# Local attention's first three slots between the MLP's last steps, and TensorE multiplying an identity in the opening

## The reference, cut to what matters

```python
def _reference_tuple_inner(inputs, ...):                 # the first layer
    x = _layernorm(inputs, ln1_g, ln1_b)
    attn_out, extra_loss = _lha_attention(x, Wq, Wk, Wv, Whq, Whk, Wo)   # 16 heads of 8
    x = attn_out + inputs
    y = _layernorm(x, ln2_g, ln2_b)
    y = jax.nn.relu(jnp.einsum('bsd,dm->bsm', y, W1) + b1)              # 128 -> 512
    y = jnp.einsum('bsm,md->bsd', y, W2) + b2
    return (x + y, extra_loss)
...
def _layer(x, wqkv, qs, ksc, wo, lg, lb, w1, b1, w2, b2):   # twice, the local layers
    h = shift_token(x)                       # half of the features from the token before
    q, k, v = jnp.split(h @ wqkv, 3, axis=-1)                            # 8 heads of 64
    q = l2norm(q) * qs
    k = l2norm(k) * ksc
    q, k = rotary_xpos(q, k)
    o = local_attention(q, k, v)             # windows of 64, each sees itself and the one before
    x = x + o @ wo
    ...                                      # shift, layer norm, gated MLP
```

## Time and profile before

| | |
|---|---|
| median of 3 runs | 1442.46 us (1438.47 to 1443.82) |
| the profiled execution | 1443.05 us, span 1441.3 us |
| mean granted TensorE clock | 0.964 of full |
| PE busy | 1268.8 us (88%) |
| DVE busy | 1084.5 us (75%) |
| ACT busy | 1007.7 us (70%) |
| POOL busy | 824.9 us (57%) |

### The profile page before, as it was taken

One profiled execution on the slowest core, in us unless ns is written; L12 is line 12 of the kernel. 1 busy time (PEld: TensorE's weight loads), 2 busy tenths in 40 slices (PEclk: granted clock), 3 DMA queues, 4 the chain that ended last, 5 costly groups with the idle time before them and its releaser, 6 DMA issues.

```text
span 1441.3 us, 27920 instructions
## 1 busy us (share of the span) xinstructions
PE 1268.8 (88%) x9636; PEld 643.8 (45%) x9636; DVE 1084.5 (75%) x1927; ACT 1007.7 (70%) x2327; POOL 824.9 (57%) x1020
## 2 busy tenths in 40 slices
PE   4489989899899977896799999988987999999898
PEld 1122222222222212365366666665434666666554
DVE  6678888888888865334499999994448999999644
ACT  4656767666676656774489999984348999999632
POOL 3466667676667631133778888860048787887100
PEclk9579999999999999998799999999999999999999
DMA  6533333333333320001111111120001111111001
GB/s 165 97 60 66 59 72 69 60 66 60 68 73 60 66 53 1 1 1 33 26 27 32 30 27 28 28 60 8 0 22 42 28 27 27 29 30 28 2 22 37
DMA packets 161119, 60.87 MB, mean 42 GB/s; under 512 B 139690, under 2 KB 152788, under 8 KB 160980
## 3 DMA queue, kind: packets, MB, share of 16 engines
q1 hardware_dynamic: 160980, 59.09, 19.3%
HBM read 8.60 MB, written 2.10 MB: 7 GB/s over the span
## 4 chain that ended last, share of the span: by engine, by line
PE 29%; ACT 11%; DVE 8%; issue 4%; POOL 2%; ACTq 0%; DVEq 0%; POOLq 0%
ACT la_s L1859 8%; PE la_ring L1480 6%; PE la_ring L1492 3%; PE la_s L1515 3%; PE la_pT L1589 3%; DVE la_prob L1748 2%; PE la_pT L1528 2%; PE la_m L1663 2%; PE la_ring L1577 2%; PE la_s L1579 1%; PE la_pT L1579 1%; PE la_s L1577 1%; ACT la_v_own L1901 1%; PE la_s L1507 1%; PE la_o L1544 1%
## 5 line engine op out<-in xcount | busy, mean ns | idle before, releaser
L785 DVE TENSOR_REDUCE row_max<-max_ps 128x2 f32<-128x1024 f32 x256 | 312.8, 1222 | 77.3 <-PE max_ps L481 75.8
L890 ACT ACTIVATE prob<-scores_ps 128x1024 f32<-128x1024 f32 x256 | 261.8, 1023 | 145.3 <-PE scores_ps L459 141.8
L1859 ACT ACTIVATE la_s<-la_s,la_bias,la_inv 128x128 f32<-128x128 f32 x512 | 223.2, 443 | 7.0 <-DVE la_bias L1736 7.0
L2010 POOL TENSOR_TENSOR la_turned<-la_raw,lw_rot 128x1024 f32<-128x1024 f32 x64 | 150.8, 2356 | 117.1 <-PE la_ring L1492 72.1
L1480 PE MATMUL la_ring<-lw_wqkv,la_hT 128*128 128x512 f32 x384 | 202.6, 638 | 15.5 <-DVE la_swapped L1711 6.8
L459 PE MATMUL scores_ps<-stack 128*128 128x512 f16 x512 | 155.7, 386 | 36.6 <-ACT prob L890 36.2
L2016 POOL TENSOR_TENSOR la_turned<-la_turned,la_swapped 128x1024 f32<-128x1024 f32 x64 | 150.6, 2354 | 5.0
L495 PE MATMUL heads_ps<-prob,XT 128*32 128x512 f32 x1024 | 137.9, 611 | 0.0
L481 PE MATMUL max_ps<-stack 24*128 24x512 f16 x512 | 102.7, 398 | 31.1 <-DVE row_max L785 19.1
L459 PEld LDWEIGHTS scores_ps<-stack 128*128 128x128 f16 x512 | 34.5, 97 | 203.8 <-ACT prob L890 148.9
L1067 POOL TENSOR_TENSOR cl<-cl,cl_inv 128x512 f32<-128x512 f32 x60 | 62.8, 1047 | 103.3 <-DVE cl_inv L691 103.3
(11 more groups left out here) (186 smaller groups left out, 2748.7 us busy)
## 6 DMA issues: line engine op xcount, KB each, us to landing
la_v_back<-la_v_own SPq DMA_DIRECT2D x112, 128.0 KB, 2.3
X<-in_x SPq DMA_DIRECT2D x8, 256.0 KB, 5.0
stack<-stack_tok SPq DMA_TRANSPOSE x128, 3.2
out<-X SPq DMA_DIRECT2D x8, 256.0 KB, 2.3
lw_wqkv<-in_wqkv SPq DMA_DIRECT2D x2, 768.0 KB, 4.3
lw_rot<-in_rot SPq DMA_DIRECT2D x2, 512.0 KB, 5.6
stack<-shift_row SPq DMA_DIRECT2D x64, 2.0 KB
lw_w<-in_fw SPq DMA_DIRECT2D x2, 341.0 KB
```

The lines of the kernel that those rows point to most:

```text
L785: nc.vector.tensor_reduce(row_max[:, grp % 2, w // 2, :, w % 2], max_ps[:], AX.X, ALU.max).then_inc(max_made, 1)
L890: nc.scalar.activation(prob[:, c % 4, 2 * pr:2 * pr + 2, :], scores_ps[:], ACT.Exp, scale=1.0 / LOGIT_SCALE).then_inc(exp_made, 1)
L1859: ins = nc.scalar.activation(s_ps[:, place(h), :], s_ps[:, place(h), :], ACT.Exp, bias=bias[:, T % 2, h:h + 1], scale=inv[:, T % 4, h:h + ...
L2010: nc.gpsimd.tensor_tensor(spun, raw[:, T % 2].rearrange("p s (h f) -> p s h f", f=LD), rot[:, T % TPB, :, 0, :].unsqueeze(2).to_broadcast( ...
```

## The change

Two edits, each of which stands alone.

**The seam.** One block is left. `local_layers` no longer opens a block but returns five programs, one per engine; each, when called, writes the engine's preparations and returns its `slot`. `run` calls the program after slot `LAYERS_OPEN` = 275 (step 0 of the MLP's round 6), and layer slots 0, 1 and 2 after slots 288, 295 and 302 (the last steps of rounds 7, 8 and 9). The others follow the MLP. SP goes on with the layers' DMAs after its own. Semaphore waits stand where the barrier was: DVE's preparations wait for the attention's last projection, the first projection for all hidden products (its banks were theirs), the first transpose of probabilities for the last sum, the first weighting for the last `take_turned`. The preparations now use SBUF that the opening's and attention's buffers gave up (`own.close()`), so `stack` is split into `even_stack`, which holds `room`, and `odd_stack`, and five of the layers' buffers (`oT`, `csq`, `hn`, `gate`, `prod`) become views of `room`.

**The opening.** `stay_busy` writes four products of `ident16` with itself (f16, 128x512) into the unused `scores_ps`, behind each `make_max_scores` and each early bench use in slots -42 to -2: 26 times. Nobody reads them. The wait for the late weight loads, `ident16` among them, moves from the first row maxima to slot -42.

```diff
+MLP_END = MLP_SLOT + MLP_STEPS * (B + 4)
+LAYERS_OPEN = MLP_SLOT + MLP_STEPS * 7
+LAYER_AT = [MLP_SLOT + MLP_STEPS * (9 + i) - 1 for i in range(3)]
+WARMING = 4
...
-        def run(slot):
-            for n in range(FIRST_SLOT, MLP_SLOT + MLP_STEPS * (B + 4)):
-                slot(n)
+        def run(both, eng, program):
+
+            for n in range(FIRST_SLOT, MLP_END):
+                both(n)
+                if n == LAYERS_OPEN:
+                    layer_slot = program(eng)
+                if n in LAYER_AT:
+                    layer_slot(LAYER_AT.index(n))
+            for n in range(len(LAYER_AT), layers["slots"]):
+                layer_slot(n)
...
-                if u == 0:
-                    pe.wait_ge(late_loaded, 16 * len(late_loads))
...
+            def stay_busy():
+
+                for i in range(WARMING):
+                    nc.tensor.matmul(scores_ps[:, i % 2, :], ident16[:],
+                                     ident16[:].unsqueeze(1).to_broadcast([P, S // P, P]), start=True, stop=True)
...
                 s, (early, late) = streams(n), bench_uses(n)
+                if tile_at_step(n, 7) == 0:
+                    pe.wait_ge(late_loaded, 16 * len(late_loads))
+                unread = 7 - LEAD_PREP <= n < -LEAD_SCORES
                 if s["max"] is not None:
                     make_max_scores(s["max"])
+                    if unread:
+                        stay_busy()
                 for use in early:
                     fill_bench(use)
+                    if unread:
+                        stay_busy()
...
-            run(both)
+            run(both, pe, layers["tensor"])
...
-        @block.tensor
-        def _(pe):
+    def tensor_program(pe):
             pe.wait_ge(ready, 1)
+        pe.wait_ge(front["early_loaded"], 16 * EARLY_LOADS)
...
                     pe.wait_ge(h_made, 2 * (b + 1))
+                if T == 0:
+                    pe.wait_ge(front["h_made"], MC * B)
...
-            run(dve, slot)
+        return slot
...
-        def _(dve):
+    def vector_program(dve):
+        dve.wait_ge(front["proj_added"], B)
             nc.vector.memset(minus_half[:], -0.5)
```

More of the change, by code:

```diff
@@ L822, in both @@
                 mlp_slot(n)
-            run(both)
+            run(both, dve, layers["vector"])
         @block.scalar
@@ L1019, in both @@
                 mlp_slot(n)
-            run(both)
+            run(both, act, layers["scalar"])
         @block.gpsimd
@@ L1140, in both @@
                 mlp_slot(n)
-            run(both)
+            run(both, pool, layers["gpsimd"])
         @block.sync
@@ L1188, in _ @@
             sp.wait_ge(early_loaded, 16 * len(early_loads))
+            layer_slot = layers["sync"](sp)
+            for n in range(layers["slots"]):
+                layer_slot(n)
+            sp.wait_ge(layers["stored"], 16 * B)
 def over(slot, last):
@@ new lines, in prob_turn @@
+        def prob_turn(T, half):
+            pe.wait_ge(shared, 2 * T + half + 1)
+            if T > 0:
+                pe.wait_ge((pT_low, pT_high)[half], T)
+            if T == 0 and half == 0:
+                pe.wait_ge(front["added"], B)
+            elif T % NT == 0 and T > 0:
+                pe.wait_ge(f_added, T // NT * B)
+            for j in range(4 * half, 4 * half + 4):
+                mm = nc.tensor.transpose(pT_ps[:, j, :], prob[:, T % 2, j, :], ident[:])
+            mm.then_inc(pT_filled, 1)
@@ new lines, in weigh @@
+        def weigh(T, half):
+            t, at = T % TPB, T % RING_TILES
+            if half == 0:
+                pe.wait_ge(v_moved[at], moves(t) * (T // RING_TILES + 1))
+                if T > 0:
+                    pe.wait_ge(oT_made, T)
+                else:
+                    pe.wait_ge(front["XT_made"], B)
+            if half == 0:
+                pe.wait_ge(pT_low, T + 1)
+                pe.wait_ge(pT_high, T + 1)
+            for pair in (2 * half, 2 * half + 1):
+                for w in range(2):
+                    for e in range(2):
+                        h = 2 * pair + e
+                        mm = nc.tensor.matmul(o_ps[64 * e:64 * e + 64, pair, 64 * w:64 * w + 64],
+                                              (v_back, v_own)[w][:, at, h, :],
+                                              probT[:, place(h), 64 * w:64 * w + 64], start=True, stop=True)
+            mm.then_inc(o_filled, 1)
@@ L1628, in slot @@
+        def slot(n):
+            T, R, U, O = (tile_at(n - x) for x in (0, 2, 3, 4))
+            f, ahead, behind, end = (ffn_at(n - x) for x in (0, -1, 1, 2))
+            if f is not None:
                 if O is not None:
                     prob_turn(O, 0)
[L1630 to L1637 removed]
@@ L1638, in slot @@
-                if R is not None:
-                    transpose(R, TURN_K)
-                b = ended(n - 7)
-                if b is not None:
-                    pe.wait_ge(csq_made, b + 1)
-                    for tile in range(TPB):
-                        mm = nc.tensor.matmul(m_ps[:, tile:tile + 1], csq[:, tile * P:(tile + 1) * P],
-                                              mean_of[:, 0:1], start=True, stop=True)
-                    mm.then_inc(m_filled, 1)
-                b = ended(n - 6)
@@ L1667, in slot @@
+                gated(f, 0)
                 if O is not None:
@@ new lines, in slot @@
+            if O is not None:
+                prob_turn(O, 0)
+            if U is not None:
+                scores(U)
+            if R is not None:
+                transpose(R, TURN_Q)
+            if O is not None:
+                prob_turn(O, 1)
+            if T is not None:
+                project(T, PROJ_V)
+            if R is not None:
+                transpose(R, TURN_K)
+            b = ended(n - 7)
+            if b is not None:
+                pe.wait_ge(csq_made, b + 1)
+                for tile in range(TPB):
+                    mm = nc.tensor.matmul(m_ps[:, tile:tile + 1], csq[:, tile * P:(tile + 1) * P],
+                                          mean_of[:, 0:1], start=True, stop=True)
+                mm.then_inc(m_filled, 1)
```

1425 lines of the change are left out of this document (696 added, 729 removed).

## The result

The changed kernel takes 1448.04 us (median of 5 runs, 1446.75 to 1451.85) where before took 1442.46 (also the median of 5 runs; the table ahead of the prediction says 3). The ratio is 1.0046, with a 95% interval of 1.0027 to 1.0065. Three executions of the experiments that took 2655 to 6520 us (one each of e1, e3 and before) count in the medians but not in the ratios, so a ratio isn't the quotient of two medians. The forecast was 1429.5, 0.9% faster, and its range ended at 1437. It was wrong: by the bound of 0.5% the kernel is level with before, on its slower side, where the forecast had a chance of 0.13 for level and 0.02 for slower.

What follows compares the result with a forecast made beforehand. The prediction took PE as the bound in the MLP and a fixed chain of waits from tile to tile in the local layers. 1442.5 - 14.3 (seam) + 1.3 (opening) = 1429.5 us; 8-in-10 range 1423 to 1437.

Steps and rivals of the forecast that it cites:

- steps 1 to 4: Seam: account from opening the layers inside the MLP to the start of `spin(3)`; 16.3 us earlier, 14.3 after deductions.
- step 1: Seam: layers open inside the MLP; PE, ACT and POOL wait for `ready` at 652.9, costing PE 3.1 us.
- step 3: Seam: POOL's base of batch 7 stands behind slot 0's spin, ending at 678.2 instead of 670.4; POOL decides the last sum.
- the mark: Start of `spin(3)` in the local layers, at 713.84 before; what it moves, the end was to move.
- The prediction's 1430.5: Seam: total if DVE's memsets were blocked beside POOL's inversion, making `ready` a microsecond later.
- run at full clock: Opening: the four slots behind the groups, 81.66 to 91.20 us, take 1.91 each instead of 9.54 together: -1.9 us.
- The rival by the rule of the Trainium skill: Opening: activity releases the throttle, so groups bring full clock at once; opening 0, total 1428.2; no chance of its own given.
- Sum: Whole kernel: median 1442.5 - 14.3 for the seam + 1.3 for the opening = 1429.5 us.
- Rival E: Opening: groups run at half clock throughout, +17 us, total 1445.2, slower than before; chance 0.04.

Runs made afterwards that it cites:

- e1: Kernel before with the opening's part of the change alone (26 groups of four f16 products and the early wait), seam untouched: 1461.91 us, ratio 1.0142.
- e3: Changed kernel with `WARMING = 0`, so the seam's part alone: 1427.70 us, ratio 0.9914.
- e8: e3 with PE's and ACT's wait for `ready` moved from the opening of the layers to their first slot: 1427.56 us, ratio 0.9913.
- e5: Changed kernel with 24 products of one column added in the opening, 256 added instructions in all: 1430.19 us, ratio 0.9934.
- e2: Kernel before with 104 products of one column (208 instructions) before the first maxima, and the early wait: 1458.74 us, ratio 1.0122.
- e4: Changed kernel with `WARMING = 5`, 260 added instructions in place of 208: 1431.87 us, ratio 0.9944.
- e10: e9 with POOL's base of the last batch (7) moved ahead of `spin(0)`: 1420.88 us, ratio 0.9848.
- e11: e10 with 40 f16 products in the opening, 18 before the first maxima and two behind each of the next 11: 1420.43 us, ratio 0.9852.
- e9: e8 with DVE's multiplication of `rot` by the gains moved one slot later, behind its shift of batch 4: 1425.67 us, ratio 0.9890.
- e6: e3 with 64 products of one column, 128 instructions: 1443.36 us, ratio 1.0021.
- e7: e3 with 40 products of one column, 80 instructions: 1428.97 us, ratio 0.9922.

## Why the prediction was wrong

**The seam, steps 1 to 4.** The mechanism held, step by step. In e3, whose MLP runs 1.95 us ahead of before's up to batch 4, the numbers with those 1.95 added are: `ready` 652.8 (forecast 652.9); PE's stop 2.87 (3.1). `spin(0)` ended at 677.4 (675.6), the last base at 680.0 (678.2), `spin(1)` started at 683.5 (681.5), `spin(2)` at 692.2 (689.8), and `spin(3)` at 701.65 (699.5). The move was 12.2 in e3 and 13.5 in after, against 14.3; the 1.3 between the two are the half clock just before `spin(3)`, in e3 and not in after. The step that was mis-sized is step 1: the stop was priced at its own 3.1 us, and cost 4.8, because PE's clock fell behind it (in e3 the next eight products took 3.14 and 2.46 us instead of 1.88 twice, 1.8 more). From there the lateness ran through all the sums (1.8 to 2.4). The prediction had half clock only after the idle time at 677.6. The gains took 3.6 us there, not 2.6; that they cost nothing held in e3 and after, where PE was late by its own stop, and no longer once that stop was gone (e8). The last base did start right behind the 4.7 us spin, as step 3 says. Its end decided the last sum: in after at 702.28, by POOL. And the mark wasn't all: the last spin came 1.6 us earlier still against before, in after as in e3.

**The memsets beside POOL.** They took no longer than in the earlier trace rows: 1.9 us from the moments to `ready` in e3. The prediction's 1430.5, with the memsets held up, had no cause here.

**The opening.** Forecast +1.3 (-1 to +4), measured +2.8 between the first and the 16th maxima in after, +2.1 in e1 and +2.2 in e5, and +0.6 for the first one's start, which varies by as much between kernels whose opening is the same. A group took 1.89 at half clock and 1.03 to 1.04 at full (forecast 1.66, and 0.83 to 1.0). The first slots of after, PE alone:

```profile
58.71 0.60 PE L492 MATMUL max_ps<-even_stack 24*128 24x512 f16 x2 [8.71 <-DMA even_stack<-stack_tok]
59.24 1.89 PE L557 MATMUL scores_ps<-ident 128*128 128x512 f16 x4
61.06 0.61 PE L492 MATMUL max_ps<-even_stack 24*128 24x512 f16 x2
...
65.47 0.39 PE L492 MATMUL max_ps<-even_stack 24*128 24x512 f16 x2
67.18 0.39 PE L492 MATMUL max_ps<-even_stack 24*128 24x512 f16 x2 [0.35 <-DVE row_max L809]
68.91 0.39 PE L492 MATMUL max_ps<-even_stack 24*128 24x512 f16 x2 [0.26 <-DVE row_max L809]
```

Half clock for the first slots, full from 64 us, lone slots at 1.7: as forecast. What failed is that the four slots behind the groups "run at full clock": after's clock was back at half from 87.9 to 94.7 us, soon after the groups end at 84.3, and these slots took 9.8 us (PE's maxima at 84.67 and 94.46) instead of the 7.6 of the forecast. The rival by the rule of the Trainium skill, TensorE: Matmul & The Clock Gate, "Part 1: The HAM clock gate" (activity releases the throttle, 0 for the opening) had the clock right from 64 to 88 us, but neither in the first five microseconds of the maxima nor behind the groups.

**What was not in the sum.** The failing step is the silent one before "Sum": everything between the opening and the seam was carried over unchanged, because no instruction there was changed. It took 14.3 us where the sum has nothing. That this equals the 14.3 forecast for the seam is chance. In the traced execution, after's slowest, the span came out 8.8 over before's where the forecast has 13.0 under it: of these 21.8, 14.3 are the attention up to the 229th maximum, 4.5 what follows up to the MLP's sums, 2.1 the opening, 0.8 the seam, and the spins' 1.6 less and 1.7 more behind the last spin all but cancel. Rival E, the only one slower than before, had another mechanism (groups at half clock throughout), which the trace refutes: full clock from 64.0 to 87.9 us. That the added instructions have a cost by their number alone was weighed nowhere. The signs were in before's profile: a queue of code transfers on the page, and in the timeline POOL waiting 0.3 to 0.9 us for 21 of the 26 groups of three transposes from 100 to 520 us, so with no slack against a late one.

The Trainium skill, Runtime: NRT & Kernel Launch, "Instruction fetch mechanics", says that an engine's code comes in blocks of 16 KiB, 256 instructions, by its own DMA queue, and calls the cost mostly hidden. The trace agrees on the size and the spacing (16 KB, one per 257 instructions of PE in the trace). It doesn't agree that the cost is hidden: e2 has it at 1.2%. What after's chain shows is not PE waiting for code, but POOL waiting for the transposes beside it. The Trainium skill, DMA: Bandwidth & Descriptors, "Queues, rings and completion order", says that a DMA engine changes between queues packet by packet, which fits the longest packet of 1.25 to 1.9 us in each group that was hit; no run here shows which engine carried it.

**What stays open.** Beyond the hits, after lost 2.9 us between the 229th and the last maximum and 1.6 up to the MLP's sums. Half clocks of 3.4 us stand there: two beside the 2.9 (from 582.8 and 593.1 us) and one beside the 1.6 (613.6). One between the 229th and the last maximum goes with 1.6 in e2, e4, e8, e10 and e11, two with 2.9 in e1 and e9, and none with nothing in e3, e5, e6 and e7. So this goes with the clock and not with the hits; what sets it off wasn't tried. Nor was a second `stack_tok` tried, which would give the casts slack at any count.

## What to carry to other kernels

Instructions added to an engine (here PE) move all its later code fetches against the work, and where a fetch meets a transfer that somebody waits for, it can cost more than the instructions do. So lay the same events of both traces side by side in the stages that the change does not touch. If they drift apart in jumps, change the count (here by filling up to 256) before judging the change. A wait that is taken off one engine shows its worth only when the queue that ended it is emptied too: e8 gave 0.7 us at the mark, e9 with the gains moved 4.0 to 5.3 more.

## What was not expected of the hardware

- PE's code comes in 16 KB packets of 0.9 to 1.8 us. One beside a group of three DMA transposes made the group 5.0 to 6.2 us long instead of 4.2. The 8 KB packets of queue 14 (0.3 to 0.7 us) left it at 4.9 at most.
- 208 PE instructions of one column each, in idle time, cost 1.2% of the kernel (e2); 80 (e7) or 256 (e5, 48 of them such, the rest the groups) cost the attention nothing that was measured.
- After a stop of PE of 2.3 us the opening had the half clock for 13 us, although PE was busy 12.2 of the next 14 (e11); after a stop of 2.87 in the MLP it lasted 3.4 us (e3).
